# Scatter pacing in the last two batches: a wait for landings before each fourth scatter instead of waits for attention steps and for each eighth

## What is computed

```python
x = x + xattn(ctx_768, layernorm(x), mask)          # 4 heads of 64
h = layernorm(x).reshape(4096, 256)
topk_idx, topk_w = route(h)                          # 8 of 64 experts
pos = running count of each expert, in token order
valid = pos < 256
buf[e, pos] = h[token]                               # only where valid
y = (silu(buf @ w_gate) * (buf @ w_up)) @ w_down
out[token] += y[e, pos] * topk_w
x = x + out
```

## Time and profile before

| | us |
|---|---|
| median of 3 runs (lowest to highest) | 1108.94 (1107.0 to 1112.97) |
| the profiled execution's own time | 1109.89 |
| its span, first to last instruction | 1108.1 |
| mean granted TensorE clock, share of full | 0.908 |
| busy PE / DVE / ACT / POOL, of the span | 892.2 / 661.7 / 463.1 / 616.9 |
| first scatter's start, last scatter's start | 257.8, 813.28 |
| first expert's rows asked for | 815.46 |

### The profile page before, as it was taken

One profiled execution on the slowest core, in us unless ns is written; L12 is line 12 of the kernel. 1 busy time (PEld: TensorE's weight loads), 2 busy tenths in 40 slices (PEclk: granted clock), 3 DMA queues, 4 the chain that ended last, 5 costly groups with the idle time before them and its releaser, 6 DMA issues.

```text
span 1108.1 us, 13512 instructions
## 1 busy us (share of the span) xinstructions
PE 892.2 (81%) x3944; PEld 636.7 (57%) x3944; DVE 661.7 (60%) x1953; ACT 463.1 (42%) x931; POOL 616.9 (56%) x571
## 2 busy tenths in 40 slices
PE   2869999989999999998999987895149999888200
PEld 1446666646666656666655545784038888777100
DVE  4485638986598886597876666756514443333106
ACT  2834675743756634757443433432013333222000
POOL 4540232303785653675564673566638888888840
PEclk9979999999999999999998996987569999999755
DMA  6829801111211322210126312100739999888689
GB/s 241 303 52 386 315 1 41 39 41 63 102 68 69 124 90 64 97 57 7 65 83 228 107 35 93 34 28 18 256 126 288 314 275 164 163 156 130 71 256 392
DMA packets 85336, 150.79 MB, mean 136 GB/s; under 512 B 14089, under 2 KB 53049, under 8 KB 83215
## 3 DMA queue, kind: packets, MB, share of 16 engines
q1 hardware_dynamic: 54543, 112.32, 29.3%
q0 software_dynamic: 30720, 37.61, 17.0%
HBM read 69.19 MB, written 97.45 MB: 150 GB/s over the span
## 4 chain that ended last, share of the span: by engine, by line
PE 57%; DVE 14%; issue 10%; DMA 7%; POOL 6%; ACT 5%; another core or an unknown queue 1%; POOLq 0%; SPq 0%; DVEq 0%; ACTq 0%
PE ps_o L1313 17%; PE ps_u L1377 5%; PE ps_s L1289 5%; PE ps_s L1291 5%; PE ps_u L1233 4%; PE ps_u L1203 4%; POOL sum L1155 3%; DMA sum<-again,row_ids 2%; PE ps_u L1325 2%; PE ps_o L1308 2%; PE ps_o L1386 2%; DVE mp L1648 2%; DMA out_rows<-again,row_ids 2%; POOL out_rows L1155 2%; DMA again<-out_rows 2%
## 5 line engine op out<-in xcount | busy, mean ns | idle before, releaser
L1080 POOL DMA_INDIRECT slot_rows<-rows,slot_idx x256 | 253.7, 991 | 199.4 <-issue 94.4
L1648 DVE TENSOR_REDUCE mp<-ps_u 128x1 f32<-128x512 f32 x256 | 164.8, 685 | 93.0 <-PE ps_u L1233 78.7
L1518 ACT ACTIVATE probs<-ps_s 128x512 f32<-128x512 f32 x256 | 139.6, 596 | 153.7 <-PE ps_s L1291 107.9
L1155 POOL DMA_INDIRECT sum<-again,row_ids x84 | 131.1, 1561 | 26.0 <-issue 22.3
L1313 PE MATMUL ps_o<-probs,pool 128*128 128x512 f32 (+1 forms) x288 | 137.8, 601 | 4.3 <-ACT den L1539 4.3
L1377 PE MATMUL ps_u<-again 128*128 128x256 f32 x512 | 123.2, 384 | 0.0
L1313 PE MATMUL ps_o<-probs,V 128*128 128x512 f32 (+1 forms) x216 | 105.4, 610 | 5.7 <-ACT probs L1521 3.8
L1820 DVE TENSOR_SCALAR again<-ps_o,again 128x256 f32<-128x256 f32 x128 | 56.0, 479 | 77.7 <-DMA sum<-again,row_ids 50.0
L1291 PE MATMUL ps_s<-qbT,Kb 65*128 65x512 f32 (+1 forms) x252 | 102.1, 405 | 0.0
L1377 PEld LDWEIGHTS ps_u<-again 128*128 128x128 f32 x512 | 94.0, 194 | 10.6
L1155 POOL DMA_INDIRECT out_rows<-again,row_ids x44 | 68.8, 1564 | 27.0 <-DVE row_ids L1821 15.1
(11 more groups left out here) (201 smaller groups left out, 1761.9 us busy)
## 6 DMA issues: line engine op xcount, KB each, us to landing
again<-in_wexp SPq DMA_DIRECT2D x64, 384.0 KB, 6.3
slot_rows<-rows SPq DMA_DIRECT2D x2, 10272.0 KB, 35.1
again<-slot_rows SPq DMA_DIRECT2D x64, 321.0 KB
sum<-rows SPq DMA_DIRECT2D x2, 4352.0 KB, 27.9
again<-sum SPq DMA_DIRECT2D x8, 1024.0 KB, 11.3
Kb<-K SPq DMA_DIRECT2D x16, 275.5 KB
pool<-in_x SPq DMA_DIRECT2D x4, 1024.0 KB, 5.2
xres<-in_x SPq DMA_DIRECT2D x8, 512.0 KB
```

What stands on the lines that cost most here:

```text
L1080: pool.indirect_dma_start(out=slot_rows, out_offset=bass.IndirectOffsetOnAxis(ap=slot_idx[x][:, q, k:k + 1], axis=0), in_=rows[x][:, q, :] ...
L1155: pool.indirect_dma_start(out=(out, *sums)[e % PLANES], out_offset=bass.IndirectOffsetOnAxis(ap=row_ids[:, e % RING, t:t + 1], axis=0), in ...
L1518: act.activation(probs[:, n % NPR, hh, :], ps_s[:, u % NSC, :], ACT.Exp).then_inc(s["probs_made"], 1)
L1648: v.tensor_reduce(mp[:, i, tile, half:half + 1], bank((*t, i))[:, :], AX.X, ALU.max).then_inc(s["emptied_vec"], 1)
```

## The change

The two constants become one table, (2, 0), (2, 1), (3, 0) and (3, 1) each with 4. `paced` no longer answers for batch 2, so its scatters wait for no step. `grouped` is true for all four halves: before scatters 4, 8, ..., 28 of a half POOL waits until all earlier ones of that half have landed. The words that go with the change say that the last two tiles go back to back; the code has (3, 1) in the table like the others, so its tiles 2 and 3 have these waits too.

```diff
--- before.py
+++ after.py
@@ -101,8 +101,7 @@
 PHASE = 2 * NKT * PR
 KEY_PACE = 4
 ROOM = 1
-GROUP = 8
-THREE_FROM = {(B - 2, 0): 107, (B - 2, 1): 119}
+GROUP = {(B - 2, 0): 4, (B - 2, 1): 4, (B - 1, 0): 4, (B - 1, 1): 4}
 
 
 LAST_MAXIMA = ((0, 12), (17, 29), (33, 50))
@@ -543,12 +542,9 @@
 
         if (b, x) < (B - 2, 0):
             return NKT * PR * (2 * b + x + 2) + (TOPK * q + k) // 2
-        if (b, x) in THREE_FROM:
-            return THREE_FROM[(b, x)] + (TOPK * q + k) // 3
-
     def grouped(self, b, x):
 
-        return (B - 2, 0) <= (b, x) < (B - 1, 1) and self.paced(b, x, 0, 0) is None
+        return (b, x) in GROUP
 
     def normed(self, at):
         b, pair = at // KEY_PAIRS, at % KEY_PAIRS
@@ -1072,10 +1068,10 @@
                     pool.wait_ge(s["rows_made"], n + 1)
                     pool.wait_ge(s["hn_made"], QT * (2 * b + x) + q + 1)
                     pool.wait_ge(s["filled"], 16 * FILLS)
-                if plan.paced(b, x, q, k) and (TOPK * q + k) % (3 if (b, x) in THREE_FROM else 2) == 0:
+                if plan.paced(b, x, q, k) and k % 2 == 0:
                     pool.wait_ge(s["values_done"], plan.paced(b, x, q, k) + 1)
                 before = TOPK * q + k
-                if plan.grouped(b, x) and before and before % GROUP == 0:
+                if plan.grouped(b, x) and before and before % GROUP[(b, x)] == 0:
                     pool.wait_ge(s[f"scattered{x}"], HALF_SCATTERS * b + 16 * before)
                 pool.indirect_dma_start(
                     out=slot_rows, out_offset=bass.IndirectOffsetOnAxis(ap=slot_idx[x][:, q, k:k + 1], axis=0),
```

## The result

| | before | after |
|---|---|---|
| median of the runs, us | 1110.95 (1107.0 to 1113.36, 4 runs) | 1125.04 (1119.17 to 1128.58, 4 runs) |
| ratio, 95% interval | 1 | 1.0121 [1.0075, 1.0168] |
| profiled execution: time, span, us | 1109.89, 1108.1 | 1126.6, 1124.8 |

The change makes the kernel slower by 1.2 per cent, 14.1 us between the medians; between the two profiled executions it is 16.7. I had forecast 1121.0.

What follows compares the result with a forecast made beforehand. POOL mostly waits for DVE's row lists, with little to spare; the last scatter's start counts. Shifts of 0.2, 0, 10.6 and 1.4 give 12.2 us on 1109.9, so 1122.1, less 1.0: forecast 1121, range 1106 to 1132.

Steps and rivals of the forecast that it cites:

- slower as the likeliest case: Whole kernel: a measured time from 1114.5 us up counts as slower; chance 0.67.
- Step 1: Batch 2 on POOL: scatters, waits, bias addition and load delays sum to 121.2 us; (3, 0) shifts by 0.2.
- The terms for the loads: Batch 2 waits under expert weight loads: 4.5 us more for the first, 3.1 each for two others.
- the gap at scatter 28: Scatter 28 of a half: existing pause and new landing wait counted as one gap, 2.1 us on average.
- Step 2: (3, 0): scatters, seven waits and the bias addition take 54.9 us; (3, 1) starts at 766.5, shift 0.
- covered by 3 us: Bias addition for (3, 1): its first tile is there at 737.5, before the projection that came at 740.73.
- Step 3: Tiles 0 and 1 of (3, 1): 34.0 us, with 6.2 from two waits under weights; tile 2 shifts by 10.6.
- Step 4: Tiles 2 and 3 of (3, 1): first to last scatter takes 24.8 us instead of 23.3, shift 1.4.
- Landings not delayed by weights: Rival: weight loads do not delay landings where it counts; shift 5.8 us, time 1115; chance 0.12.
- no change: Rival: other engines set free, waits at 2.1 us, weights delay little or nothing; time 1107 or 1110; chance 0.18.
- Dearer waits: Rival: each wait 0.3 us more, plus 1.8 at scatter 28 four times; shift 27.8, time 1137; chance 0.10.
- The faster one: Rival: groups of four free the other engines, waits about 1.5 us, undelayed by weights; 10.5 us earlier, 1098; chance 0.10.

Runs made afterwards that it cites:

- the runs with 1.23 and 1.71 us: The change with each landing wait replaced by small fills of an unused tile on POOL: three (1.23 us pause), ratio 0.9891; six (1.71 us), 0.9897.
- one fill: The change with each landing wait replaced by one small fill of an unused tile on POOL, a pause of 0.90 us: ratio 0.9963.

## Why the prediction was right, and where it was not

The forecast of 1121 for 1125.04, with slower as the likeliest case, came out by its own mechanism: landing waits on POOL that nothing hides in (3, 1). Going by the steps, in the trace of the change:

- Step 1, batch 2: 715.04 - 592.05 = 123.0 us for the 121.2 of the sum. The terms for the loads were good: gaps of 6.08, 5.30 and 4.85, for 6.6, 5.2 and 5.2. Mis-sized was one term, the gap at scatter 28: "At scatter 28 I count one gap, since the pause and the wait want the same landings." It is 3.00 and 2.68 here, 2.66 and 2.68 in batch 3, while the neighbours are 1.9 to 2.2: 0.6 to 0.9 us on top of the 2.1, four times. The start was 2.15 us later than I had taken it, by DVE's list at 591.05; that list starts between 589.1 and 591.9 in the other edited kernels, with the same instructions ahead of it, and at 591.93 where batch 2 was left as before, so this is no effect of the change. So (3, 0) was 4.1 late and not 0.2.
- Step 2, (3, 0): 54.8 us for 54.9. Its shift was not 0 but 3.3, since POOL came later and the list no longer mattered. One sentence failed: the projection behind the bias addition was to be "covered by 3 us". It waited 12.48 us: DVE's work ahead of it was done 11 us earlier (a list at 728.45 for 739.47), and the addition started 3.4 us later than I had it. It cost nothing at the end, as POOL was behind by 7 us (769.85 against the 762.7 that the list would have allowed).
- Step 3, tiles 0 and 1 of (3, 1): 804.26 - 769.85 = 34.4 for 34.0. The two waits under the weights, 5.87 and 5.21, are 7.2 of the 16.2 us, and the run with the weights moved shows their cause. The sign did not rest on them alone: the last scatter of that run, at 820.92, is still 7.6 us behind 813.28.
- Step 4: 25.2 for 24.8, the scatter 28 again.

Together 16.2 for 12.2 us, of which 2.2 are the late start and the rest, 1.8, is less than what scatter 28 added. Without the late start it is 14.0, close to the 14.1 between the medians. One reading behind the terms for the loads was wrong: the start at 602.06 in the kernel before ended a wait for an attention step, as its row says (PE's L1313), so only the packets until 601 spoke for the weights.

```profile
602.06 0.98 POOL L1080 DMA_INDIRECT slot_rows<-rows,slot_idx  x1 [7.42 <-PE ps_o L1313]
```

The Trainium skill, "DMA: Bandwidth & Descriptors", section "Anatomy of one DMA — SWDGE (gpsimd) path", has about 2.0 us of fixed cost that scales with nothing; the quiet gaps agree, those of 4.85 to 6.08 don't.

The rivals. "Landings not delayed by weights" fell with the 5.87 and 5.21, and "no change" with it, since it needed weights that delay little. "Dearer waits" was right that the pause at scatter 28 and the wait don't overlap wholly, but for 0.6 to 0.9 us and not 1.8; the other quiet waits are no dearer than 2.1 on average. The faster one was half right, and it is the better half of this study. The engines were set free, lists came 3.8 to 8.7 us earlier, and ACT's three idle times without a releaser are gone: between 650 and 770 the longest such is

```profile
691.72 1.09 ACT L1514 ACTIVATE probs<-ps_s 128x512 f32<-128x512 f32 x2 [2.47 <-issue]
```

Its condition was that waits take 1.5 us and are not delayed under weights. Landing waits can't do that; fills can, and the runs with 1.23 and 1.71 us came to 0.9891 and 0.9897: the first is 1098.8 us on the 1110.95 of before, where I had worked out 1098. That fit is partly luck: the interval is 5.9 us to either side. The last scatters say the same more surely: 801.23 and 808.72, around the 802.8 worked out for 1.5 us.

## What to carry to other kernels

A wait has a reason and a price, and the two can be parted: here the pause was wanted and the landing was paid for. Where a wait helps engines that don't depend on what it waits for, try a pause of fixed length, from long to short, until the others fall behind. And put nothing that waits for a small transfer under a large load when that engine is the one that sets the end.

## What was not expected of the hardware

A run of scatters holds the other engines up only after some of them. In the run without waits in (3, 1), L1727 and L1728 on DVE are 0.21 us apart at 774.22, eight scatters behind POOL's last pause (before 764.20), and L660 and L661 still 0.19 at 777.74; at 798.39 the former are 1.42 apart. The Trainium skill, "SBUF — State Buffer", section "SBUF: two separate sides", lets, of the engines, only VectorE and GpSimd block each other, whichever has the shared port, for the length of one instruction; by that the early steps should have been held like the late ones, and 14.77 us with a gap of 0.3 us behind every scatter should not occur. The trace differs from it, or something else is at work; PE and ACT stood as well, for 11.52 and 14.31 us.

Per scatter, with the pause in, a group of four took (595.88 - 590.13) / 4 = 1.44 us with one fill, where the engines fell behind, and (598.13 - 592.05) / 4 = 1.52 with three, where they did not. A queue behind POOL that empties at a rate between the two would explain the sudden difference and the late onset.

What comes late can be read from the run without waits in batch 2. PE's projection ends, as the trace models it, at 608.80 + 1.13 = 609.93, and DVE adds it at 631.27, 21.3 us later; in the changed kernel the same two are 0.03 us apart (608.72 and 608.75). The scores that ACT takes at 620.10 ended at 607.64, 12.5 us earlier. In the run without waits in (3, 1) DVE waits up to 1.24 us for its own step before. The work is done, and the signal of it, or the taking of the signal, comes late, the later the longer scatters run. The scatters' own packets don't pile up meanwhile: the scatter queue has 464 from 616 to 628 us, for nine scatters of 48 each. What holds the signals stays open.

A landing under a load of weights takes 5.34 us instead of 2.13, and the pause that POOL makes by itself at scatter 28 of a half of batches 2 and 3, 1.96 to 2.09 us where no wait or fill stands (2.77 once), does not hide a landing wait in it: with one the gap is 2.66 to 3.01.
